# A first pass in software-pipelined turns: its four order tables rewritten, and the router's transpose moved to another PSUM buffer

## The reference, cut to what matters

```python
# layer 0, cross attention: 16 heads of 8, 77 keys from ctx, a relative-position bias, masked keys
x = x + xattn(layernorm(x), ctx, mask, Wq, Wk, Wv, Wo, rel_emb)        # steps "x0"
# layer 0, ffn block: its input is layernorm(x), and its result is added to x
h = layernorm(x)
h = h + attn(layernorm(h)*ln1_w+ln1_b)   # depthwise conv over 3 tokens, rotary q and k, causal softmax: steps "f0"
logits = (layernorm(h)*ln2_w+ln2_b) @ router_w ; expert = argmax(logits)     # steps "fc"
# each token then goes through one of 4 experts, in a later pass, from a table of rows sorted by expert
```

## Time and profile before

| | |
|---|---|
| median of 3 runs | 3064.12 us (3061.4 to 3073.03) |
| the profiled execution | 3070.26 us, span 3068.5 us |
| granted clock of PE, whole span | 0.957 of full speed |
| 100 to 1000 us of the span: busy | PE 846.17, DVE 832.68, ACT 821.17, POOL 384.20 us |
| the same stretch, granted clock | 1.00 |

### The profile page before, as it was taken

The page is one execution under the profiler, slowest core; times in us unless marked ns, Lnnn a source line. Parts: engine busy times, 40 slices in busy tenths (PEclk is TensorE's granted clock), DMA queues, the critical chain, the costliest instruction groups (busy, mean ns, idle before and its releaser), DMA issues. The chain is left out here.

```text
span 3068.5 us, 78311 instructions
## 1 busy us (share of the span) xinstructions
PE 2755.7 (90%) x28313; PEld 1958.0 (64%) x28313; DVE 2595.8 (85%) x6995; ACT 2420.2 (79%) x6105; POOL 1027.2 (33%) x1693
## 2 busy tenths in 40 slices
PE   6999999999999669979999997976799999999997
PEld 4666666666666446657777775332667777777776
DVE  5899999999999426459999995798499999999996
ACT  3899989999999435547777774498499999999995
POOL 1344444444444200035555552000034444444441
PEclk8999999999999679989999997998899999999998
DMA  1012121111111021101111110000300000000000
GB/s 49 27 34 62 51 38 34 35 34 35 34 34 33 14 61 43 42 21 35 34 34 34 34 35 25 12 0 0 105 9 16 16 16 16 16 16 16 16 16 9
DMA packets 177630, 91.15 MB, mean 30 GB/s; under 512 B 46339, under 2 KB 174021, under 8 KB 177251
## 3 DMA queue, kind: packets, MB, share of 16 engines
q1 hardware_dynamic: 171716, 76.85, 9.3%
q0 software_dynamic: 4096, 8.40, 0.8%
q10 hardware_dynamic: 1440, 0.90, 0.1%
HBM read 43.73 MB, written 42.36 MB: 28 GB/s over the span
## 5 line engine op out<-in xcount | busy, mean ns | idle before, releaser
L2336 DVE TENSOR_TENSOR th<-tf 128x2048 f32<-128x2048 f32 (+1 forms) x256 | 574.1, 2243 | 6.6 <-ACT cg L2139 6.6
L2168 ACT ACTIVATE th<-th 128x2048 f32<-128x2048 f32 (+1 forms) x256 | 481.6, 1883 | 0.6 <-DVE th L2336 0.6
L652 ACT ACTIVATE probf<-probf,colf 128x128 f32<-128x128 f32 x1024 | 313.2, 393 | 0.0
L2116 POOL TENSOR_SCALAR colf<-colf 128x1 f32<-128x1 f32 x64 | 134.8, 2107 | 441.0 <-DVE colf L2317 441.0
L2230 PE MATMUL p_rho<-th,late_w_row 128*32 128x128 f32 x8064 | 277.5, 276 | 2.5 <-ACT th L2168 2.3
L2230 PEld LDWEIGHTS p_rho<-th,late_w_row 128*32 128x32 f32 x8064 | 209.3, 110 | 26.7 <-ACT th L2168 3.6
L1765 PE MATMUL acc<-xnT_all,wT 128*128 128x512 f32 x384 | 181.3, 625 | 29.6 <-DVE tmax L1957 13.2
L2179 ACT ACTIVATE tl<-tf 128x128 f32<-128x128 f32 x640 | 199.6, 391 | 0.0
L656 ACT COPY probTf<-fp 128x1024 f32<-128x1024 f32 x128 | 129.5, 1012 | 45.7 <-PE fp L800 45.7
L800 PE MATMUL fp<-ident,probf 128*128 128x128 f32 x1024 | 142.4, 284 | 23.6 <-ACT ygf L659 20.5
L747 PE MATMUL xp<-ident,prob 128*77 128x128 f32 x1024 | 142.3, 283 | 20.8 <-DVE colc L993 19.4
(11 more groups left out here) (437 smaller groups left out, 8543.1 us busy)
## 6 DMA issues: line engine op xcount, KB each, us to landing
rows<-zeros SPq DMA_DIRECT2D x64, 256.0 KB, 2.4
cxT<-in_ctxT SPq DMA_DIRECT2D x128, 38.5 KB, 1.9
xb<-rows SPq DMA_DIRECT2D x67, 64.0 KB, 1.8
rows<-yb SPq DMA_DIRECT2D x67, 64.0 KB, 1.5
x<-in_x SPq DMA_DIRECT2D x64, 64.0 KB, 1.8
x_mid<-x SPq DMA_DIRECT2D x64, 64.0 KB, 1.5
z<-x_mid SPq DMA_DIRECT2D x64, 64.0 KB
x_next<-z SPq DMA_DIRECT2D x64, 64.0 KB, 1.5
```

The lines of the kernel that those rows point to most:

```text
L652: last = nc.scalar.activation(scores, scores, ACT.Exp, bias=colf[s][:, 16 + HALF * hf + h:17 + HALF * hf + h])
L2168: nc.scalar.activation(b, b, ACT.Tanh).then_inc(act_done, ACT_L.did(f"t{c}.tanh", e))
L2336: nc.vector.tensor_tensor(th[i % NT][:, 0:shape[1], :], tf[s][:, CHUNK[n]:CHUNK[n + 1]].unsqueeze(2).to_broadcast(shape), tf[s][:, FEAT:FE ...
```

## The change

It does four things. The four lists are written anew (other places, and other distances between elements). In the PE list each half of f0's scores now stands beside the opposite half of x0's: f0b.S with x0a.S, as before, and also f0a.S with x0b.S. The router's transpose goes from fp bank 0 to fs bank 1, with waits to match: fc.T waits until f0a.add has read the scores in fs, fc.route follows it without a wait on DVE's f0b.add, and f0b.S waits for fc.eq and fc.slot, where f0a.S did. f0a.PT waits for f0.x of the element before instead of fc.xT. And x0.kblk, fc.scatter, fc.eps, fc.rstd and f0.kblk now stand in this order on POOL, with f0.eps and f0.rstd behind them. No instruction is added or taken away.

```diff
--- before.py
+++ after.py
@@ -140,22 +140,22 @@
 F0_BEHIND = 2
 ROUTE_BEHIND = 2
 RANK_BEHIND = 2
+ACT_A = """
+    f0a.yg@5 f0.xT@3 x0b.PTc@2 fc.xT@6 f0b.PTc@5 x0b.yg@2 x0a.exp@1 f0b.yg@5 f0.v@3 x0.xT x0.yT@2 x0b.exp@1 x0.v
+    f0.yT@5 f0a.exp@4 x0a.PTc@1 f0a.PTc@4 x0a.yg@1 f0b.exp@4
+"""
+DVE_A = """
+    x0.rden@3 x0.y@3 x0b.less@2 fc.max@7 f0.rden@6 fc.eq@7 f0.y@6 fc.first@7 fc.pick@7 fc.taken@7 x0.kT@1 x0.qT@1
+    fc.slot@7 fc.slot_i@7 x0.x@3 f0.stats@3 f0.x@6 f0.aggr@3 fc.stats@6 fc.aggr@6 f0.qk@4 f0b.add@5 x0a.add@1
+    f0b.max@5 fc.norm@6 f0.h@3 f0.norm@3 x0b.add@1 f0a.add@4 x0a.max@1 f0.conv2@3 x0b.max@1 f0.conv1@3 x0.stats
+    f0.conv0@3 x0.aggr f0a.max@4 x0.norm f0.rope@3
+"""
 PE_A = """
-    fc.rank@6 x0.o@2 f0.o@5 x0.T x0a.PT@1 f0a.S@3 x0.qkv fc.T@5 x0a.PV@1 f0a.PT@4 f0b.S@3 x0a.S x0b.PT@1 f0a.PV@4
-    x0b.S f0b.PT@4 x0b.PV@1 f0.T@2 fc.route@5 f0b.PV@4 x0.ygT@1 f0.ygT@4 f0.qkv@2 x0.yT@1 f0.yT@4
-"""
-ACT_A = """
-    f0.yT@5 f0a.exp@4 f0.v@3 x0.xT x0a.PTc@1 fc.xT@5 x0.v x0b.exp@1 x0a.yg@1 f0a.PTc@4 f0b.exp@4 f0a.yg@4 x0b.PTc@1
-    f0b.PTc@4 f0.xT@2 x0b.yg@1 f0b.yg@4 x0a.exp x0.yT@1
-"""
-DVE_A = """
-    f0a.max@4 x0a.add@1 f0.h@3 f0b.add@4 f0.norm@3 x0a.max@1 x0b.add@1 x0b.max@1 fc.max@6 fc.eq@6 f0.conv2@3
-    f0.conv1@3 x0.stats f0.conv0@3 x0.aggr fc.first@6 f0.rden@5 fc.pick@6 x0.rden@2 f0.y@5 x0.y@2 fc.taken@6 x0.norm
-    f0.rope@3 f0.qk@3 x0.x@2 fc.slot@6 f0.x@5 f0.stats@2 fc.stats@5 fc.slot_i@6 f0.aggr@2 fc.aggr@5 x0b.less@1
-    fc.norm@5 f0a.add@3 x0.kT x0.qT f0b.max@4
+    f0.o@6 f0b.S@5 x0a.S@1 x0a.PT@2 f0a.PT@5 x0a.PV@2 f0a.S@4 x0b.S@1 x0b.PT@2 f0a.PV@5 f0.T@3 fc.T@6 f0b.PT@5
+    x0b.PV@2 fc.route@6 f0.qkv@3 x0.ygT@2 f0b.PV@5 x0.T x0.yT@2 f0.ygT@5 x0.qkv f0.yT@5 fc.rank@6 x0.o@2
 """
 POOL_A = """
-    fc.eps@6 fc.rstd@6 fc.scatter@7 x0.kblk@1 fc.z@6 f0.eps@3 f0.rstd@3 x0.eps x0.rstd f0.kblk@3
+    fc.z@6 f0.eps@3 f0.rstd@3 x0.eps x0.rstd x0.kblk fc.scatter@6 fc.eps@5 fc.rstd@5 f0.kblk@3
 """
 ACT_B = """
     b.y@4 b.hT@3 b.tanh@1 b.xT
@@ -661,7 +661,7 @@
                 return chain
 
             def fc(e):
-                xT("fc", e, xncT[e % NF], fp[:, 0, 0:TOK], 2)
+                xT("fc", e, xncT[e % NF], fs[:, 1, 0:TOK], 2)
                 yield
 
             for dst, src in weight_loads[0::2]:
@@ -777,12 +777,12 @@
                         pe.wait_ge(pool_done, POOL_L.value("f0.kblk", e))
                         if e >= 1:
                             pe.wait_ge(dve_done, DVE_L.value("f0b.add", e - 1))
-                        if e >= 1 + ROUTE_BEHIND:
-                            pe.wait_ge(dve_done, DVE_L.value("fc.eq", e - 1 - ROUTE_BEHIND))
-                        if e >= 1 + RANK_BEHIND:
-                            pe.wait_ge(dve_done, DVE_L.value("fc.slot", e - 1 - RANK_BEHIND))
                     else:
                         pe.wait_ge(dve_done, DVE_L.value("f0a.add", e))
+                        if e >= ROUTE_BEHIND:
+                            pe.wait_ge(dve_done, DVE_L.value("fc.eq", e - ROUTE_BEHIND))
+                        if e >= RANK_BEHIND:
+                            pe.wait_ge(dve_done, DVE_L.value("fc.slot", e - RANK_BEHIND))
                     for b in range(2):
                         g0 = (2 * hf + b) * GROUP * HDIM
                         last = nc.tensor.matmul(fs[:, b, :], qTf[s][g0:g0 + GROUP * HDIM, :], kblkf[s][g0:g0 + GROUP * HDIM, :, :],
@@ -792,9 +792,9 @@
                     pe.wait_ge(act_done, ACT_L.value(f"{p}.exp", e))
                     if hf == 1:
                         pe.wait_ge(act_done, ACT_L.value("f0a.yg", e))
-                    elif e >= 1:
-                        pe.wait_ge(act_done, ACT_L.value("fc.xT", e - 1))
-                    if hf == 0:
+                    else:
+                        if e >= 1:
+                            pe.wait_ge(dve_done, DVE_L.value("f0.x", e - 1))
                         pe.wait_ge(act_done, ACT_L.value("f0.v", e))
                     for h in range(HALF):
                         last = nc.tensor.transpose(fp[:, h // GROUP, (h % GROUP) * TOK:(h % GROUP + 1) * TOK], probf[s][:, hf, h * TOK:(h + 1) * TOK], ident[:])
@@ -807,10 +807,15 @@
             def fc(e):
                 s = e % NF
                 pe.wait_ge(dve_done, DVE_L.value("fc.norm", e))
-                nc.tensor.transpose(fp[:, 0, 0:TOK], xnc[s][:], ident[:]).then_inc(pe_done, PE_L.did("fc.T", e))
+                if e + ROUTE_BEHIND <= LAST:
+                    pe.wait_ge(dve_done, DVE_L.value("f0a.add", e + ROUTE_BEHIND))
+                else:
+                    pe.wait_ge(dve_done, DVE_L.value("f0b.add", LAST))
+                if e >= 1:
+                    pe.wait_ge(act_done, ACT_L.value("fc.xT", e - 1))
+                nc.tensor.transpose(fs[:, 1, 0:TOK], xnc[s][:], ident[:]).then_inc(pe_done, PE_L.did("fc.T", e))
                 yield
                 pe.wait_ge(act_done, ACT_L.value("fc.xT", e))
-                pe.wait_ge(dve_done, DVE_L.value("f0b.add", min(e + ROUTE_BEHIND, LAST)))
                 if e >= 1:
                     pe.wait_ge(dve_done, DVE_L.value("fc.eq", e - 1))
                 if e >= 1 + RANK_BEHIND - ROUTE_BEHIND:
@@ -820,7 +825,10 @@
                 pe.wait_ge(dve_done, DVE_L.value("fc.taken", e))
                 pe.wait_ge(dve_done, DVE_L.value("fc.pick", e))
                 pe.wait_ge(dve_done, DVE_L.value("fc.eq", min(e + RANK_BEHIND - ROUTE_BEHIND, LAST)))
-                pe.wait_ge(dve_done, DVE_L.value("f0b.add", min(e + RANK_BEHIND, LAST)))
+                if e + RANK_BEHIND <= LAST:
+                    pe.wait_ge(dve_done, DVE_L.value("f0a.add", e + RANK_BEHIND))
+                else:
+                    pe.wait_ge(dve_done, DVE_L.value("f0b.add", LAST))
                 if e >= 1:
                     pe.wait_ge(dve_done, DVE_L.value("fc.slot", e - 1))
                 rank = fs[:, 0, 8:8 + MOE0]
```

More of the change, by code:

```diff
@@ L142 @@
 RANK_BEHIND = 2
-PE_A = """
-    fc.rank@6 x0.o@2 f0.o@5 x0.T x0a.PT@1 f0a.S@3 x0.qkv fc.T@5 x0a.PV@1 f0a.PT@4 f0b.S@3 x0a.S x0b.PT@1 f0a.PV@4
-    x0b.S f0b.PT@4 x0b.PV@1 f0.T@2 fc.route@5 f0b.PV@4 x0.ygT@1 f0.ygT@4 f0.qkv@2 x0.yT@1 f0.yT@4
-"""
 ACT_A = """
-    f0.yT@5 f0a.exp@4 f0.v@3 x0.xT x0a.PTc@1 fc.xT@5 x0.v x0b.exp@1 x0a.yg@1 f0a.PTc@4 f0b.exp@4 f0a.yg@4 x0b.PTc@1
-    f0b.PTc@4 f0.xT@2 x0b.yg@1 f0b.yg@4 x0a.exp x0.yT@1
+    f0a.yg@5 f0.xT@3 x0b.PTc@2 fc.xT@6 f0b.PTc@5 x0b.yg@2 x0a.exp@1 f0b.yg@5 f0.v@3 x0.xT x0.yT@2 x0b.exp@1 x0.v
+    f0.yT@5 f0a.exp@4 x0a.PTc@1 f0a.PTc@4 x0a.yg@1 f0b.exp@4
 """
 DVE_A = """
-    f0a.max@4 x0a.add@1 f0.h@3 f0b.add@4 f0.norm@3 x0a.max@1 x0b.add@1 x0b.max@1 fc.max@6 fc.eq@6 f0.conv2@3
-    f0.conv1@3 x0.stats f0.conv0@3 x0.aggr fc.first@6 f0.rden@5 fc.pick@6 x0.rden@2 f0.y@5 x0.y@2 fc.taken@6 x0.norm
-    f0.rope@3 f0.qk@3 x0.x@2 fc.slot@6 f0.x@5 f0.stats@2 fc.stats@5 fc.slot_i@6 f0.aggr@2 fc.aggr@5 x0b.less@1
-    fc.norm@5 f0a.add@3 x0.kT x0.qT f0b.max@4
+    x0.rden@3 x0.y@3 x0b.less@2 fc.max@7 f0.rden@6 fc.eq@7 f0.y@6 fc.first@7 fc.pick@7 fc.taken@7 x0.kT@1 x0.qT@1
[3 more added lines that the diff above has]
+"""
+PE_A = """
+    f0.o@6 f0b.S@5 x0a.S@1 x0a.PT@2 f0a.PT@5 x0a.PV@2 f0a.S@4 x0b.S@1 x0b.PT@2 f0a.PV@5 f0.T@3 fc.T@6 f0b.PT@5
+    x0b.PV@2 fc.route@6 f0.qkv@3 x0.ygT@2 f0b.PV@5 x0.T x0.yT@2 f0.ygT@5 x0.qkv f0.yT@5 fc.rank@6 x0.o@2
 """
 POOL_A = """
-    fc.eps@6 fc.rstd@6 fc.scatter@7 x0.kblk@1 fc.z@6 f0.eps@3 f0.rstd@3 x0.eps x0.rstd f0.kblk@3
+    fc.z@6 f0.eps@3 f0.rstd@3 x0.eps x0.rstd x0.kblk fc.scatter@6 fc.eps@5 fc.rstd@5 f0.kblk@3
 """
```

## The result

The changed kernel took 3076.44 us, the median of 19 runs (3068.91 to 3079.11). The kernel before, run beside it on the same chips, took 3070.47 us (19 runs, 3061.4 to 3075.56). The medians lie 6.0 us apart; the ratio of the runs is 1.0018, with a 95% interval of 1.0011 to 1.0025, which is 5.5 us slower, and within the 0.5% that I had called no change. The profiled execution took 3074.02 us, of which the span is 3072.2.

A forecast was written before the change was run, and what follows sets the result against it. The bound was taken to be the loop f0.x, routing, next f0a.PT, at 15.31 us a turn. Steady turns +9 and drain -5 gave +4 us, 3074 profiled and 3068 us as median; range 3036 to 3086.

The forecast's parts named there:

- The new turn: Steady state: POOL's 6.29 us plus 9.20 us for the rest, taken as 15.45 us against 15.31, +9 us over 64 turns.
- The drain: Last turns, after x0 has run out: 1.7 us less in each of about three, -5 us.
- the fill: First turns of the pass: set at nothing, with 5 us either way.
- a wait before f0.h: On DVE, for POOL's f0.rstd: 0.4 to 0.7 us in each turn, while fc.norm's 0.77 us wait goes.
- The eight steps: POOL from x0.kblk to f0.rstd, between DVE's x0.kT and f0.h: 5.95 us, 6.29 with releases.
- DVE's rest: From f0.h round to x0.kT: 8.93 us of DVE plus waits of 0.09 and 0.18, 9.20 us.
- f0.rden's wait: On DVE before f0.rden, with x0.yT now ahead of f0.ygT on PE: 0.18 us, about 0.2 a turn.
- The lock: DVE's f0.qk could hold POOL's fc.eps by 0.1 us, at worst 0.46; set to nothing; slower rival, chance 0.17.
- Loads late: Rival: one store in four is slow and delays x0.stats by up to 0.5 us, +8 us; within the 0.50 case.
- The loop through fp: Kernel before: f0.x, routing, the next element's f0a.PT, its halves, f0.x again; named the present bound of the 15.31 us turn.
- pairing at nothing: On PE, f0a.S beside x0b.S saves at most 0.79 us of matmul time; costed at nothing for PE's waits before x0.qkv.
- The faster rival: POOL is not the loop; one through ACT from f0b.exp sets 14.92 us a turn, 3034 us in all; chance 0.22.

The follow-up runs named there:

- e3: Changed kernel with one extra one-column instruction on POOL ahead of f0.eps, 0.25 us from start to start: 3089.38 us, ratio 1.0049 to the kernel before.
- e2: Changed kernel with the scatter moved behind f0.rstd in POOL's list: 3077.2 us, ratio 1.0014 to the kernel before.
- e9: Kernel before with x0b.less moved behind fc.norm in DVE's list: 3082.92 us, ratio 1.0029 to the kernel before.
- e14: Changed kernel with fc.z moved behind f0.rstd in POOL's list: 3089.28 us, ratio 1.0061 to the kernel before.
- e5: Kernel before with only the routing chain moved from fp to fs, its steps set back in the lists: 3086.38 us, ratio 1.0046 to the kernel before.
- e6: Kernel before with fc.norm moved behind f0a.add in DVE's list: 3130.2 us, ratio 1.0181 to the kernel before.
- e4: Changed kernel with f0a.S put behind x0b.PT in PE's list, no longer beside x0b.S: 3107.39 us, ratio 1.0108 to the kernel before.
- e1: Changed kernel with f0.h and f0.norm moved behind x0b.add in DVE's list: 3071.24 us, ratio 0.9993 to the kernel before.
- e10: Changed kernel with fc.eq and fc.first ahead of f0.rden and fc.pick before f0.y in DVE's list: 3069.97 us, ratio 0.9994 to the kernel before.
- e11: Changed kernel with the edits of e1 and e10 together: 3072.53 us, ratio 1.0004 to the kernel before.

## Why the prediction was right, and where it was not

**The size and the sign of the sum.** +4 us was forecast, +5.5 measured. The new turn came out at 15.42 us where I took 15.45, and the old at 15.30 (I had 15.31); so the steady state cost 6.9 us and not 9. The drain gave 4.4 us back where I had 5: a turn in the drain is 15.8 us long (f0's last copy at 1037.87 and 1053.66) and was 17.2 (1045.48 and 1062.64). These two terms stand. That the total came so close is in part luck: the pass by itself ended 7.0 us later, as the fill cost 4.4 that I had at nothing, and the unchanged rest was 3 us shorter in this pair of profiles.

**The wait moved, not removed.** The forecast of a wait before f0.h of 0.4 to 0.7 us, in place of fc.norm's 0.77, is met by 0.38, just under its lower end. e3 shows that the loop is closed: 0.25 us more on POOL, 0.25 more in the middle turn. The eight steps took 5.72 us where I had 5.95, and DVE's rest 9.34 where I had 9.20 (574.94, 581.02 and 590.36 in DVE's timeline); two errors of opposite sign, -0.21 and +0.14 us with the releases. f0.rden's wait of 0.27 was forecast as 0.18 to 0.2, for another reason: I took f0.ygT to be late by x0.yT ahead of it on PE. In the trace f0.ygT's load starts 0.11 us after ACT's copy f0b.yg ends (573.24), and from there the steps go back without a gap over f0b.PV and x0.ygT to f0.qkv, which waits for DVE's f0.conv0. So the part of the loop that I called DVE's runs from f0.conv0 to f0.rden over PE and ACT:

```profile
570.41 1.16 PE L766 MATMUL xs<-hcT,w_at 128*128 128x128 f32 x8 [0.18 <-DVE hcT L938]
```

```profile
573.35 0.42 PEld L684 LDWEIGHTS fp<-ident,ygf 128*128 128x128 f32 x4 [0.16 <-ACT ygf L659]
```

**The lock.** At "it could be held by 0.1; at worst 0.46" the measured fc.eps is 0.25 us against 0.22 of an undisturbed one: 0.03. In e2, where it starts beside f0.qk's second step, it is 0.37. e9 shows the same instruction at 0.22 us once x0b.less doesn't lie beside it, against 0.68; that the two-operand step on DVE holds it is thus shown for the kernel before. In the Trainium skill, "SBUF — State Buffer", section "SBUF: two separate sides", the lock is taken for a whole instruction by either side; fc.eps agrees for a step of DVE that holds one of POOL. The scatter, by which that rule was to make 0.1 to 0.2 us more, held nothing: f0.qk's two steps took 0.26 and 0.28 us, and they began at 576.96 and 577.13 while the scatter was on POOL until 577.21.

**Loads late** was to cost up to 8 us and cost nearly nothing in the changed kernel, a few turns of 15.6 to 15.7 us. e14 shows how near it was: fc.z later by three small steps, and it costs more than the wait removed.

**The wrong step: "This is the present bound."** The loop through fp was not the one thing that set 15.31 us. e5, which takes routing out of it, gained nothing, though its moved steps cost something too. A second loop was as long: DVE's list with its wait for fc.rstd as far as x0b.add, then f0.T, f0b.PV, f0b.yg and f0.ygT back to f0.rden. e9 lengthens this one and the turn grows; e6, which makes fc.T later, lost 0.94 us a turn (middle turns). In the kernel before both arrive at f0b.PV within 0.1 us. The forecast didn't suffer, as the new loop was summed by itself and the old one stood as a measured length; but I would have forecast wrongly any version that only freed fp.

**Mis-sized: the fill.** "The fill is at nothing, with 5 us either way": it was +4.4 us. PE's granted clock from 60 to 100 us was 0.96 of full speed against 0.83 in the kernel before, so the clock isn't the cause. The trace shows where it comes from: at 18 us the two kernels are within 0.1 us of each other, and one turn later x0b.add is 4.26 us behind. The kernel before, then the changed one:

```profile
35.38 0.80 DVE L896 TENSOR_TENSOR prob<-xs,bias 128x616 f32<-128x616 f32 x1 [0.26 <-PE xs L737]
```

```profile
39.64 0.80 DVE L904 TENSOR_TENSOR prob<-xs,bias 128x616 f32<-128x616 f32 x1 [4.88 <-PE xs L737]
```

In the new PE list x0b.S stands behind x0a.PT and x0a.PV of the element before (33.85 and 36.93), with ACT's copy between them, and in the second turn there is no other work to fill this. I had compared how long an element stays in the pipe, and not how full the first turns are. No run moved x0b.S, so this is read from the trace and not tried.

**Mis-sized: pairing at nothing.** Taking the pair apart costs 0.45 us a turn (e4). I had reasoned from PE's idle time before x0.qkv, which lies elsewhere in the turn. In the changed kernel PE's long wait, 0.83 us before fc.T, comes behind these scores and not ahead of them.

**The faster rival's number.** Had POOL been hidden, 3034 us would have been wrong: e1, in which f0.h doesn't wait, has 15.31 us a turn and 3071.24 in all. The loop behind POOL's isn't ACT's of 14.92 but one through PE's scores and transposes near 15.3.

**Still open.** Why e14's undisturbed turns (15.13) are shorter than e1's (15.28), though neither waits at f0.h: they differ in DVE's order, so x0b.add's place may matter, but it wasn't separated. Which of the two loops of the kernel before is the longer, by less than 0.1 us. Why e10 and e11 gained a half and nothing; their new waits are seen, the loops behind them not summed. How the drain's 4.4 us divide between the router's place and the pairs.
